# A recommendation model on one core: six look-up jobs of two tiles in place of four, and one memset in GpSimd's pauses in place of three

## The reference

```python
sp_emb = emb_tables[fidx, sp_input]            # 2048 x 26 x 32
lin_vals = lin_tables[fidx, sp_input, 0]
lin_output = ds_input @ lin_w.T + lin_b + jnp.sum(lin_vals, axis=1, keepdims=True)
s = jnp.sum(sp_emb, axis=1)
bi_pooled = 0.5 * (s * s - jnp.sum(sp_emb * sp_emb, axis=1))
x = jnp.concatenate([bi_pooled, ds_input], axis=1)
h = jax.nn.relu(x @ w1.T + b1)
h = jax.nn.relu(h @ w2.T + b2)
out = jax.nn.sigmoid(h @ fw.T + fb + lin_output)
```

## Time and profile before

| | us |
|---|---|
| median of 3 runs (lowest, highest) | 413.21 (412.94, 413.29) |
| the profiled execution's own time | 413.37 |
| its span, first to last instruction | 411.6 |
| PE busy | 405.3 (98%) |
| DVE busy | 356.2 (87%) |
| ACT busy | 279.8 (68%) |
| POOL busy | 303.0 (74%) |
| mean granted TensorE clock | 0.999 of 2.4 GHz |

### The profile page before, as it was taken

One profiled execution on the slowest core, in us unless ns is written; L12 is line 12 of the kernel. 1 busy time (PEld: TensorE's weight loads), 2 busy tenths in 40 slices (PEclk: granted clock), 3 DMA queues, 4 the chain that ended last, 5 costly groups with the idle time before them and its releaser, 6 DMA issues.

```text
span 411.6 us, 5945 instructions
## 1 busy us (share of the span) xinstructions
PE 405.3 (98%) x1910; PEld 347.3 (84%) x1910; DVE 356.2 (87%) x389; ACT 279.8 (68%) x500; POOL 303.0 (74%) x388
## 2 busy tenths in 40 slices
PE   7999999999999999998999999999999999999997
PEld 4888888888888888887888888888888887667764
DVE  7989999979699797879779999979779999989863
ACT  6999959555597655772975498767654786772243
POOL 5777778777777777876877787776777787676760
PEclk9999999999999999999999999999999999999999
DMA  8442251113311331215111512251115111101110
GB/s 216 113 152 28 27 179 28 26 24 98 117 28 20 92 122 18 27 15 186 28 22 21 188 27 31 41 179 24 18 26 180 24 15 13 12 12 12 13 13 0
DMA packets 17471, 24.85 MB, mean 60 GB/s; under 512 B 6061, under 2 KB 16399, under 8 KB 16402
## 3 DMA queue, kind: packets, MB, share of 16 engines
q1 hardware_dynamic: 8160, 19.55, 14.5%
q0 software_dynamic: 9280, 4.92, 10.9%
HBM read 24.40 MB, written 0.05 MB: 59 GB/s over the span
## 4 chain that ended last, share of the span: by engine, by line
PE 95%; ACT 2%; DVE 1%; issue 1%; DMA 1%; SPq 0%; DVEq 0%; ACTq 0%
PE cand L920 45%; PE cand L923 44%; PE bank_b L967 1%; DMA stage<-tabs 1%; PE cand L967 1%; PE bank_b L942 1%; PE bank_b L977 1%; PE bank_b L983 1%; PE cand L977 1%; ACT gates L746 0%; ACT high L713 0%; DVE masked L508 0%; PE bank_b L1106 0%; PE bank_a L942 0%; ACT h L799 0%
## 5 line engine op out<-in xcount | busy, mean ns | idle before, releaser
L388 POOL DMA_INDIRECT rows<-table,row_idx x285 | 273.2, 959 | 93.3 <-issue 64.2
L920 PE MATMUL cand<-high,gates 128*128 128x462 f32 x882 | 331.1, 375 | 2.3 <-DVE low L495 1.2
L923 PE MATMUL cand<-low,gates 128*128 128x462 f32 x882 | 328.8, 373 | 0.0
L920 PEld LDWEIGHTS cand<-high,gates 128*128 128x128 f32 x882 | 166.3, 189 | 28.8 <-issue 8.5
L923 PEld LDWEIGHTS cand<-low,gates 128*128 128x128 f32 x882 | 166.0, 188 | 19.9 <-issue 0.7
L516 DVE TENSOR_REDUCE picks<-masked 128x66 f32<-128x924 f32 x60 | 115.3, 1922 | 2.1
L508 DVE TENSOR_TENSOR masked<-cand,mask 128x924 f32<-128x924 f32 x62 | 69.3, 1118 | 32.3 <-PE cand L923 31.8
L746 ACT ACTIVATE gates<-distance,one 128x512 fp32r<-128x512 bf16 (+1 forms) x144 | 90.6, 680 | 0.0
L738 ACT ACTIVATE distance<-codes,minus_key 128x512 bf16<-128x512 f16 (+1 forms) x135 | 85.0, 680 | 0.1
L726 ACT COPY bank_b<-high 128x462 f32<-128x462 f32 x54 | 29.6, 549 | 50.6 <-DVE low L495 49.4
L483 DVE TENSOR_SCALAR gates<-bank_a,key_of 128x512 fp32r<-128x512 f32 (+1 forms) x94 | 60.9, 700 | 0.0
(11 more groups left out here) (118 smaller groups left out, 127.5 us busy)
## 6 DMA issues: line engine op xcount, KB each, us to landing
stage<-tabs SPq DMA_DIRECT2D x8, 1617.0 KB, 7.1
rows<-table,row_idx POOLq DMA_INDIRECT x285
codes<-codes_dram SPq DMA_DIRECT2D x27, 128.0 KB, 2.9
stage<-tabs SPq DMA_DIRECT2D x7, 231.0 KB, 4.6
codes<-codes_dram SPq DMA_DIRECT2D x5, 64.0 KB, 7.1
idx_raw<-sparse SPq DMA_DIRECT2D x1, 208.0 KB, 6.2
w_sb<-w2t SPq DMA_DIRECT2D x1, 128.0 KB
dense_sb<-dense_cols SPq DMA_DIRECT2D x1, 120.0 KB
```

What stands on the lines that cost most here:

```text
L388: pool.indirect_dma_start(out=to, out_offset=None, in_=table[:, :], in_offset=bass.IndirectOffsetOnAxis(ap=row_idx[:, at:at + 1], axis=0), ...
L920: first = nc.tensor.matmul(to, gate, high[f % 2][:, k, :], start=(k == 0), stop=False)
L923: last = nc.tensor.matmul(to, gate, low[f % 2][:, k, :], start=False, stop=(k == CHUNKS - 1))
```

## The change

Three edits, all in the tables and in POOL's loop. `CUT` gets two more entries, (1, 10) and (6, 2): field 1 is no longer looked up for tiles 10 and 11, field 6 no longer for tiles 2 and 3; jobs 6 and 24 shrink from four tiles to two. So 122 look-ups are left of 126, and there are 294 gathers in place of 290. (The other two lines of the list only change places.) The permits in `LET_OF` for jobs 1 to 29 go from 122 and 96 hundredths for a tile's two halves to 129 and 101. And before every ninth gather POOL clears one scratch tensor in place of three.

```diff
-    CUT = [(2, 0), (3, 12), (5, 6), (4, 8)]
+    CUT = [(1, 10), (2, 0), (3, 12), (4, 8), (5, 6), (6, 2)]
...
-    LET_OF = [[30, 30, 30, 440, 40, 40, 40, 340]] + [[122, 96] * n for n in SIZE[1:NJ - 4]] + [[140] * 8, [140] * 8, [140] * 8, [240] * 4]
+    LET_OF = [[30, 30, 30, 440, 40, 40, 40, 340]] + [[129, 101] * n for n in SIZE[1:NJ - 4]] + [[140] * 8, [140] * 8, [140] * 8, [240] * 4]
...
                         if n == 36:
                             pool.wait_ge(codes_out, 16)
                         else:
-                            pool.wait_ge(rested, 3 * ((n - 36) // 9))
-                        for used in (col_raw, col_wrap, col_hi):
-                            pool.memset(used[:, :], 0).then_inc(rested, 1)
+                            pool.wait_ge(rested, (n - 36) // 9)
+                        pool.memset(col_raw[:, :], 0).then_inc(rested, 1)
```

## The result

The changed kernel takes 401.52 us (median of 4 runs, 401.47 to 402.02); the kernel before, beside it, 413.14 (412.94 to 413.29). The ratio is 0.9722, 95% interval 0.9705 to 0.9739: 11.6 us less, where 401.5 was forecast. The profiled execution took 402.02, span 399.9, and before 413.37, span 411.6, so the spans differ by 11.7.

A forecast was written before the change was run, and what follows sets the result against it. PE, busy almost without a gap, was taken to bound the kernel. From the profiled 413.37 us, 11.79 us of matmuls came off and all else cost zero: 401.6, or 401.4 against the median, stated as 401.5; range 400.9 to 403.0.

The forecast's parts named there:

- PE's term: Jobs 6 and 24 on PE lose two tiles each: 56 matmuls, 5.90 + 5.89 = 11.79 us, all on the path.
- The estimate by the formula of the Trainium skill: PE's matmul spacing as N / 2.4 + 2.5 ns, 195 ns: 56 matmuls worth 10.9 us, kernel near 402.4; given no chance.
- Steps 6 and 24 at zero: DVE's work during the two shortened jobs runs late but costs PE nothing, covered by third `cand` buffer and gates made ahead.
- The stall at job 16: PE's existing wait for a `low` chunk, 1.47 us extra, stays: the preceding short job is the last of its field.
- the new counts lean on the shorter pause: POOL with three memsets per pause would issue tile 10's last gather at 276, making its rows 4.4 us late.
- The second rival: POOL's gathers give nothing back, nine still taking 11.93 us: last gather near 393, time 403 to 406; chance 5%.
- POOL's slack: Rows for the last squares land 3.2 us before ACT takes them, before and after the change.
- The last gather's own terms: At the kernel's end: 3.2 us to spare, and 6 us later issue (393 against 387) if pauses give nothing back.
- The sum for tile 10: 205 gathers ahead of tile 10's last: issued about 267, landed 269.4, wanted by ACT at 274.0, 4.6 us to spare.
- The slower rival: POOL's gathers become slow without the longer pause: one in nine of nearly double length, time 421 us; chance 2%.

The follow-up runs named there:

- The single cut: Changed kernel without its second new cut (6, 2), permits 126 and 98, one memset per pause: 407.16 us.
- the seventh one: Changed kernel with field 3's cut at tiles 4-5, field 6 also cut for tiles 8-9: 394.69 us with one memset per pause, 394.18 us without pause.
- the run with the moved cut: Changed kernel with field 3's cut moved from tiles 12 and 13 (job 15) to tiles 4 and 5 (job 13): 399.98 us.
- eight cuts: Changed kernel with field 3's cut at tiles 4-5, further cuts at field 6 tiles 8-9 and field 2 tiles 10-11, no pause: 391.93 us.

## Why the prediction was right

*PE's term.* 11.79 us by the jobs' own stretches; 11.7 between the spans, 11.6 between the medians. The single cut (5.9 and 5.6) and the seventh one (5.3 and 5.8, with and without the memset) give the same price once more. The spacing of 0.2105 us that the trace showed held; 28 matmuls of a short job take 5.89. The estimate by the formula of the Trainium skill (TensorE: Matmul & The Clock Gate, "Back-to-back issue gap"), 402.4, lies outside the runs, if only by 0.4 us; the rows, 210 ns where it gives 195, decide against it.

*Steps 6 and 24 at zero.* Forecast: the chunk 1.9 us early, job 7's pair 2.9 us late, job 25's 3.7. Found: 2.0, 2.7, and 3.5 (277.03 in DVE's timeline for a pair ready at 273.6). The cover of step 6 is real and has the size that was named: a chunk that comes 1.0 us later disappears in it, one that comes 3.3 later doesn't. At step 24 DVE could be 2.8 us later still without any loss, by the run with three memsets. That it is the third `cand` buffer and the gates made ahead that cover both is read from the order of the kernel; no run took them away.

*The stall at job 16.* Forecast to stay, and it stayed; the reason given, the place of the short job within its field, is shown by moving it.

*POOL.* 386.55 for the last gather against 387.0; a pause 0.50 shorter. That the new counts lean on the shorter pause is shown by the run with three memsets, 404.93. The second rival gave 404.4 for that pace, but its condition, that POOL takes the time of the memsets for itself, isn't met.

*What was wrong in it.* I held POOL's slack to be that of the last gather, 3.2 us. The wait that comes first stands earlier: tile 14's rows for ACT in job 32. In the changed kernel the last of them is issued at 364.17, landed at 366.6, and squared at 372.01, 5.4 us to spare; with three memsets it is issued at 372.10, 7.9 later. The last gather's own terms were both too small: it has 4.2 us to spare, not 3.2 (the 404.42 of the earlier trace rows is the first of the squares of the last rows, not that of the last one), and with three memsets it comes 8.2 later, not 6. That 6 less 3.2 and the measured 3.4 agree on some 3 us of loss is luck.

The sum for tile 10 has a miscount. It has 203 gathers ahead of its last one, not 205: 4 + 3 + 203 x 1.25 + 19 x 0.19 is 264.4, and 264.46 was measured where the prediction said 267. ACT squares these rows at 274.06, so 7.2 us were to spare and not 4.6. The conclusion doesn't change by it: with three memsets ACT waits 3.5 us, where 4.4 was said.

*The slower rival.* Its condition, long gathers once the pause is short, isn't met even with no pause at all. Its formula can be held against the run with five memsets, whose last gather comes at 413.60, 14.8 later than 398.79: 413.4 + 14.8 - 3.2 = 425.0, where 423.8 was measured. Seven gathers of the changed kernel take more than 1 us, all of them in the first 50 us, ahead of any pause. One starts at 48.07 and takes 1.40 us, while DVE's mask instruction, which reads two tensors in SBUF, runs (from 47.97, 0.68 us). The gather at 29.17, which had begun 0.39 us ahead of the same instruction (29.56), takes 0.94. The rule of the Trainium skill that was put beside this rival (SBUF — State Buffer, "SBUF: two separate sides"), by which VectorE and GpSimd share a port pair and the one that starts first keeps it for its whole instruction, fits both. For a VectorE instruction with two inputs in SBUF the page says so only against a GpSimd operation that reads SBUF; a gather reads its row numbers there. None of this was tested by itself.

## What to carry to other kernels

Work taken off an engine that is busy without a gap is worth its spacing in the trace, start to start, as long as each neighbour's slack is held against the first reader that would wait. A short step in a software pipeline costs nothing by being short; it costs where something that the next stage reads early stands in it behind a wait. The slack of a background queue has to be taken at each of its consumers, and the smallest one counts, wherever it stands.

## What wasn't expected of the hardware

A gather's rows can come far later than the 2.4 us from issue to landing of the earlier trace rows. In the run with the moved cut tile 6's last gather is issued at 175.86, SP issues a 1.6 MB load of `stage` at 176.39, and ACT gets the rows only at 181.81, 5.9 us after issue. ACT's timeline, SP's, and the stretch (266 GB/s, DMA engines 80% busy, 14% before it):

```profile
181.81 0.71 ACT L771 ACTIVATE squares<-rows 128x608 f32<-128x608 f32 x1 [5.32 <-DMA rows<-table,row_idx]
```

```profile
176.39 0.33 SPq L338 DMA_DIRECT2D stage<-tabs  x1
```

```profile
172.00:176.00 4.00, 4.00 (x21) 3.57 (x20) 3.96 (x5) 3.97 (x8) 2.98 (x4) 1.00 0.14 13
176.00:182.00 6.00, 6.00 (x30) 5.39 (x29) 5.46 (x7) 0.68 (x2) 4.92 (x6) 1.00 0.80 266
```

It isn't the only case. With eight cuts tile 6's rows reach ACT 6.0 us after the last issue (the load issued 1.9 before it), with tile 10's sums moved 5.4 (3.1 before), and tile 11's 4.75 (2.9 before); with five memsets tile 4's take 4.05 and tile 6's 4.7, again with a load close by. Where ACT waited for rows and no load had been issued in the 8 us before the last gather or 1 us after it, they took 2.3 to 2.5, but for two (3.5 and 3.9), whose cause is open.

A slack of less than some 6 us for rows that are gathered when a table is loaded is therefore less than it looks; in the run with the moved cut PE lost nothing by it. No run took the load away, so that it is the load that delays the gather is read from the times, not shown.
